# Attention values of one item packed into one PSUM bank, in a two-block decoder on one core

## The reference, cut to what matters

```
scores = einsum('nqhd,nkhd->nhqk', q, k) + bias          # 16 heads of 8 features
attn   = softmax(scores * scale, axis=-1)
out    = einsum('nhqk,nkhd->nqhd', attn, v)               # the part that changes
x      = layernorm(x + out.reshape(n, q, 128) @ Wo.T + bo)
```

## Time and profile before

| What | Value |
|---|---|
| Time, median of 3 runs | 1018.94 us (1016.09, 1018.94, 1019.32) |
| Profiled execution, span | 1016.3 us; the profile gives nothing around it |
| Granted TensorE clock over the span | 0.839 |
| TensorE matmul busy | 787.6 us, 77% of the span |
| VectorE busy | 628.6 us, 62% |
| ScalarE busy | 508.2 us, 50% |
| GpSimd busy | 182.5 us, 18% |
| Context transposes (line 662) | 272, 60.3 us busy |
| Evacuations (line 704) | 144, 51.9 us busy |
| Reciprocals (line 768) | 68, 17.3 us busy |

### The profile page before, as it was taken

The page is one execution under the profiler, slowest core; times in us unless marked ns, Lnnn a source line. Parts: engine busy times, 40 slices in busy tenths (PEclk is TensorE's granted clock), DMA queues, the critical chain, the costliest instruction groups (busy, mean ns, idle before and its releaser), DMA issues.

```text
span 1016.3 us, 20624 instructions
## 1 busy us (share of the span) xinstructions
PE 787.6 (77%) x7086; PEld 426.8 (42%) x7109; DVE 628.6 (62%) x2000; ACT 508.2 (50%) x867; POOL 182.5 (18%) x313
## 2 busy tenths in 40 slices
PE   2787898889996638866659999559999846999960
PEld 1232333444443414443413334313333435999950
DVE  2587987676755814246268994368887345555567
ACT  1157786556564312406417876506566524666630
POOL 2241211011110201001301110121000032602324
PEclk8698998999997765767658999659999957999985
DMA  5466541322120222001522210152110151212212
GB/s 131 114 203 177 155 119 49 115 64 64 51 81 1 63 63 50 2 1 47 140 63 71 73 35 2 37 132 68 51 49 3 57 216 40 90 48 60 75 46 66
DMA packets 76074, 75.57 MB, mean 74 GB/s; under 512 B 21376, under 2 KB 65152, under 8 KB 75216
## 3 DMA queue, kind: packets, MB, share of 16 engines
q1 hardware_dynamic: 73504, 67.18, 23.3%
q0 software_dynamic: 2480, 7.21, 2.1%
HBM read 50.66 MB, written 23.13 MB: 73 GB/s over the span
## 4 chain that ended last, share of the span: by engine, by line
PE 62%; DVE 18%; issue 6%; ACT 4%; POOL 4%; DMA 4%; SPq 2%; POOLq 0%; DVEq 0%; ACTq 0%
PE PS L648 12%; PE PS L582 12%; PE PS L1807 8%; PE PS L599 7%; DVE MS L753 5%; PE PS L662 4%; PE PS L1817 4%; PE PS L589 3%; PE PS L326 2%; POOL experts_x L1718 1%; PE PS L1012 1%; DVE Y L748 1%; DVE CX L770 1%; ACT X L1047 1%; PE PS L173 1%
## 5 line engine op out<-in xcount | busy, mean ns | idle before, releaser
L753 DVE TENSOR_REDUCE MS<-PS 128x2 f32<-128x512 f32 (+2 forms) x448 | 249.2, 591 | 122.1 <-PE PS L599 68.2
L711 ACT ACTIVATE BIG<-PS 128x1024 f32<-128x1024 f32 (+2 forms) x288 | 260.0, 907 | 85.5 <-PE PS L589 45.2
L582 PE MATMUL PS<-BIG 62*128 62x256 bf16 (+1 forms) x1088 | 205.9, 285 | 91.8 <-DVE MS L753 30.4
L589 PE MATMUL PS<-BIG 64*128 64x256 bf16 (+1 forms) x1088 | 187.1, 273 | 1.3 <-DMA BIG<-MT 1.3
L648 PE MATMUL PS<-BIG,VA 128*32 128x256 f32 (+1 forms) x2176 | 170.1, 386 | 1.8 <-ACT OT L704 1.8
L582 PEld LDWEIGHTS PS<-BIG 62*128 62x128 bf16 x1088 | 68.1, 96 | 235.6 <-issue 120.5
L704 ACT COPY OT<-PS 128x256 f32<-128x256 f32 (+1 forms) x144 | 51.9, 360 | 106.1 <-PE PS L648 106.1
L1807 PE MATMUL PS<-OT,VA 128*128 128x128 f32 x736 | 96.3, 278 | 0.4 <-ACT OT L1864 0.4
L1807 PEld LDWEIGHTS PS<-OT,VA 128*128 128x128 f32 x736 | 91.0, 195 | 0.7 <-ACT OT L1864 0.7
L817 POOL CAST MB<-MS 128x16 bf16<-128x16 f32 (+1 forms) x72 | 16.0, 222 | 383.0 <-DVE MS L753 191.8
L648 PEld LDWEIGHTS PS<-BIG,VA 128*32 128x32 f32 x2176 | 43.8, 110 | 73.6 <-issue 63.2
(11 more groups left out here) (223 smaller groups left out, 1091.8 us busy)
## 6 DMA issues: line engine op xcount, KB each, us to landing
rows_q<-parts SPq DMA_DIRECT2D x32, 192.0 KB, 2.1
rows_k<-parts SPq DMA_DIRECT2D x32, 192.0 KB, 2.1
BIG<-rows_q SPq DMA_DIRECT2D x64, 96.0 KB
BIG<-rows_k SPq DMA_DIRECT2D x64, 96.0 KB
BIG<-in_ex_w SPq DMA_DIRECT2D x3, 2048.0 KB, 11.8
BIG<-rows_q SPq DMA_DIRECT2D x64, 64.0 KB
BIG<-rows_k SPq DMA_DIRECT2D x64, 64.0 KB
OT<-experts_x SPq DMA_DIRECT2D x46, 64.0 KB
```

What stands on the lines that cost most here:

```text
L582: return nc.tensor.matmul(bank[:, first:first + kw], g.Q6[b.buf][rows, u, qt * P:(qt + 1) * P], g.K6[b.buf][rows, u, 0:kw], start=start, s ...
L589: return nc.tensor.matmul(g.bank[2 * (v % 2) + a][:, core.offset[kt]:core.offset[kt] + n], g.K6[b.buf][rows, v, kt * P:(kt + 1) * P], g.Q6 ...
L711: nc.scalar.activation(g.PT[v // 2 % 2][:, 2 * (v % 2):2 * (v % 2) + 2, 0:w], g.bank2[v % 2][:, :, 0:w], ACT.Exp, scale=SCALE).then_inc(se ...
L753: nc.vector.tensor_reduce(g.MS[:, 0:n, a, u], self.ring_bank["mx", step, a][:, 0:n * w] .rearrange("p (n k) -> p n k", n=n), axis=AX_X, op ...
```

## The change

`values` now writes group `grp` with `q, o = divmod(grp, 2)`. `o` picks the half of bank 6's columns. `q` picks the half of the 32 partitions: the heads 8 to 15 of `VA` have their 9 filled columns at 16 to 24 of the 32, where heads 0 to 7 have zeros, so groups 2 and 3 are accumulated on the same columns as groups 0 and 1. Only the very first matmul of an item starts the accumulation. One copy evacuates the whole bank per item; only group 0 of the next item waits for it. The transposes are 2 per block of queries, 4 for an item, in steps 0 and 1. The context is one step per item: one reciprocal of 32 (16 in f0), then one multiply per block of queries. The order of heads in V's columns is changed on the host (`VFIRST`) to fit.

```diff
 def contexts(self, no):
-        return self.g.line.cx_done.at(self.items[no].cx + self.nqt)
+        return self.g.line.cx_done.at(self.items[no].k + 1)
 def turns_of(self, items, step):
         k, n = divmod(step - self.LAG - 14, 8)
-        b = self.item(items, k)
-        qt, half = {0: (0, 0), 1: (0, 1), 3: (1, 0), 4: (1, 1)}.get(n, (2, 0))
-        return (b, qt, half) if b and qt < b.core.nqt else (None, 0, 0)
+        return (self.item(items, k), n) if n < 2 else (None, 0)
 # values
-                after(pe, self.ot_done, n)
+                if grp == 0:
+                    after(pe, self.ot_done, b.k)
             lo, w = core.queries[kt]
+            q, o = divmod(grp, 2)
             for hh in range(4):
                 last = nc.tensor.matmul(
-                    g.bank[6][PVW * hh:PVW * hh + PVW, lo:lo + w],
-                    g.VA[b.par][:, kt, 8 * (hh % 2) + 2 * grp + hh // 2, :],
+                    g.bank[6][PVW * hh:PVW * hh + PVW, S * o + lo:S * o + lo + w],
+                    g.VA[b.par][:, kt, 8 * q + 4 * (hh % 2) + 2 * o + hh // 2, :],
                     g.PT[grp % 2][:, hh, core.offset[kt]:core.offset[kt] + w],
-                    start=kt == 0, stop=kt == core.nqt - 1)
+                    start=grp == 0 and kt == 0, stop=grp == 3 and kt == core.nqt - 1, skip_group_check=True)
-        def turn_context(b, qt, half):
-            if half == 0:
-                pe.wait_ge(*self.ot_done.at(4 * b.k + 4))
-                self.bank7(pe, self.cx_done.at(b.cx + qt + 1))
-            for grp in (2 * half, 2 * half + 1):
-                last = nc.tensor.transpose(g.bank[7][:, grp * P:(grp + 1) * P], g.OT[b.par][:, grp, qt * P:(qt + 1) * P],
-                                           g.ident[:, :])
-            if half == 1:
+        def turn_context(b, qt):
+            if qt == 0:
+                pe.wait_ge(*self.ot_done.at(b.k + 1))
+                self.bank7(pe, self.cx_done.at(b.k + 1))
+            if qt >= b.core.nqt:
+                return
+            for o in range(2):
+                last = nc.tensor.transpose(g.bank[7][:, (2 * qt + o) * P:(2 * qt + o + 1) * P],
+                                           g.OT[b.par][:, o, qt * P:(qt + 1) * P], g.ident[:, :])
+            if qt == b.core.nqt - 1:
                 last.then_inc(self.cxt_ready.sem, 1)
-        def evacuate(n):
-            act.wait_ge(*self.pv_done.at(n + 1))
-            if grp == 0 and b.k >= 2:
-                after(act, self.cxt_ready, self.items[b.k - 1].cx)
+        def evacuate(b):
+            act.wait_ge(*self.pv_done.at(4 * b.k + 4))
+            after(act, self.cxt_ready, b.k - 1)
             w = b.core.nqt * P
-            nc.scalar.copy(g.OT[b.par][:, grp, 0:w], g.bank[6][:, 0:w]).then_inc(self.ot_done.sem, 1)
+            nc.scalar.copy(g.OT[b.par][:, 0:2, 0:w], g.bank[6].rearrange("p (o t) -> p o t", o=2)[:, :, 0:w])\
+              .then_inc(self.ot_done.sem, 1)
-            if v % 2 == 0:
-                evacuate(v // 2 - 2)
+            if v % 8 == 2 and self.item(items, v // 8 - 1):
+                evacuate(self.items[v // 8 - 1])
-        def context(b, qt):
+        def context(b):
+            nqt = b.core.nqt
+            dve.wait_ge(*self.cxt_ready.at(b.k + 1))
+            sums = g.bank[7][:, 0:nqt * H * W2].rearrange("p (n w) -> p n w", w=W2)
+            rsum = g.rsum[:, 0:nqt * H]
+            nc.vector.reciprocal(rsum, sums[:, :, DH]).then_inc(self.chain.sem, 1)
+            dve.wait_ge(*self.chain.at(b.k + 1))
+            for qt in range(nqt):
+                heads = slice(qt * H, (qt + 1) * H)
+                last = nc.vector.tensor_tensor(
+                    g.CX[:, b.no * nqt + qt, :].rearrange("p (d s r) -> p r s d", d=DH, r=4),
+                    sums[:, heads, 0:DH].rearrange("p (r s) d -> p r s d", s=4),
+                    rsum[:, heads].rearrange("p (r s) -> p r s", s=4).unsqueeze(3).to_broadcast([P, 4, 4, DH]), ALU.mult)
+            last.then_inc(self.cx_done.sem, 1)
 # value_rows, GpSimd
+            for q in range(2):
+                heads = slice(8 * q, 8 * q + 8)
+                to = g.VA[b.par][:, 0:nqt, heads, W2 * q:W2 * q + DH]
+                if bias is None:
+                    last = nc.gpsimd.tensor_copy(to, v[:, :, heads, :])
+                    continue
+                row = bias.rearrange("p (d h) -> p h d", d=DH)[:, heads, :]
                 for n in range(nqt):
-                    last = nc.gpsimd.tensor_tensor(to[:, n, :, :], v[:, n, :, :], row, ALU.add)
+                    last = nc.gpsimd.tensor_tensor(to[:, n, :, :], v[:, n, heads, :], row, ALU.add)
+            last.then_inc(self.va_ready.sem, 1)
 # start of the program, GpSimd
             for buf in g.VA:
-                last = nc.gpsimd.memset(buf[:, :, :, DH:DH + 1], 1.0)
+                for q in range(2):
+                    last = nc.gpsimd.memset(buf[:, :, 8 * q:8 * q + 8, W2 * q + DH:W2 * q + DH + 1], 1.0)
 # host: the columns of the V weights, of a1's V bias and of ctx
+VFIRST = DFIRST.reshape(DH, 2, 2, 4).transpose(0, 2, 1, 3).reshape(-1)
```

More of the change, by code:

```diff
@@ L48 @@
 PVW = 32
+W2 = PVW // 2
 NPARTS = 4
@@ L510, in __init__ @@
         self.feat_total = [0] * NBUF
-        self.cx_total = self.joins = 0
+        self.joins = 0
         self.bank7_read = None
@@ L538, in add @@
             self.feat_total[b.buf] += 16 * core.loads(no)
-            b.feat, b.cx, b.joins = self.feat_total[b.buf], self.cx_total, self.joins
-            self.cx_total += core.nqt
+            b.feat, b.joins = self.feat_total[b.buf], self.joins
             self.joins += 2 if core.causal else 0
@@ L686, in tensor @@
                 turn_m(b, half)
-            b, qt, half = self.turns_of(items, step)
+            b, qt = self.turns_of(items, step)
             if b:
-                turn_context(b, qt, half)
+                turn_context(b, qt)
             if side:
@@ L778, in vector @@
                     join(bm, step % 8 // 4)
-            b, qt, half = self.turns_of(items, step)
-            if b and half == 1:
-                context(b, qt)
+            b, turn = self.turns_of(items, step)
+            if b and turn == 1:
+                context(b)
             if side:
@@ L796, in value_rows @@
             b.core.values_ready(pool, b.no)
-            to = g.VA[b.par][:, 0:nqt, :, 0:DH]
             v = b.core.values[:, b.no * nqt:(b.no + 1) * nqt, :].rearrange("p t (d h) -> p t h d", d=DH)
-            if bias is None:
-                nc.gpsimd.tensor_copy(to, v).then_inc(self.va_ready.sem, 1)
-            else:
-                row = bias.rearrange("p (d h) -> p h d", d=DH)
+            for q in range(2):
[5 more added lines that the diff above has]
+                row = bias.rearrange("p (d h) -> p h d", d=DH)[:, heads, :]
                 for n in range(nqt):
-                    last = nc.gpsimd.tensor_tensor(to[:, n, :, :], v[:, n, :, :], row, ALU.add)
-                last.then_inc(self.va_ready.sem, 1)
+                    last = nc.gpsimd.tensor_tensor(to[:, n, :, :], v[:, n, heads, :], row, ALU.add)
+            last.then_inc(self.va_ready.sem, 1)
         def parts_of_m(b, half):
@@ L1994, in allocate @@
         self.MT = [sb(f"MT_{i}", [16, S], BF16) for i in range(2)]
-        self.rsum = sb("rsum", [P, H])
+        self.rsum = sb("rsum", [P, 2 * H])
         self.fbuf = [sb(f"fbuf{i}", [P, CH]) for i in range(2)]
@@ L2600, in layout @@
     for n in w:
-        w[n] = w[n][DFIRST] if n in ("a0_qa", "a0_qb", "a0_ka", "a0_kb") else w[n][DFIRST][:, DFIRST]
+        w[n] = w[n][DFIRST] if n in ("a0_qa", "a0_qb", "a0_ka", "a0_kb") else w[n][DFIRST][:, VFIRST if n[3:] == "v" else DFIRST]
     io["weights"] = np.stack([w[n] for n in WEIGHTS], axis=1)
@@ L2606, in layout @@
     rows = {"a1_bv": a["L1_attn_bv"], "a1_bo": a["L1_attn_bo"], "x1_bo": a["L1_xattn_bo"]}
-    io["rowvecs"] = np.repeat(np.stack([rows[n][DFIRST] for n in ROWVECS])[None], P, axis=0)
+    io["rowvecs"] = np.repeat(np.stack([rows[n][VFIRST if n == "a1_bv" else DFIRST] for n in ROWVECS])[None], P, axis=0)
     io["router"] = np.repeat(a["L0_ffn_w_router"][DFIRST][:, None], P, axis=1)
@@ L2624, in layout @@
     io["xt"] = io["x"].T
-    io["ctx"] = a["ctx_1024"].reshape(T, D)[:, DFIRST]
-    io["ctxt"] = io["ctx"].T
+    ctx = a["ctx_1024"].reshape(T, D)
+    io["ctx"], io["ctxt"] = ctx[:, VFIRST], ctx[:, DFIRST].T
     return io
```

3 lines of the change are left out of this document (removed).

## The result

The changed kernel takes 1012.57 us (median of 20 runs, 1007.24 to 1019.92) against 1019.32 (20 runs, 1014.57 to 1029.36) for the kernel before: ratio 0.9935, interval [0.9914, 0.9956]. That is 6.7 us faster where 24 were forecast, outside the range. The profiled execution spans 1008.1 us, the one before 1016.3: two single executions, 8.2 us apart.

A forecast was written before the change was run, and what follows sets the result against it. TensorE was taken to bound the attention stages, sharing a1 with VectorE. Transposes 15.6, context 1.5 and tails 7.8, less 1.0 for the evacuation wait, gave 23.9 us off the 1018.94 median: 995 us, range 985 to 1007.

The forecast's parts named there:

- Transposes: In the attention stages and f0, halving the transposes takes off half of line 662's share of the chain: 15.6 us.
- Context on VectorE: One reciprocal of 32 columns at 0.27 us replaces two of 16; half its chain share in a1 and x1 saves 1.5 us.
- Evacuation wait: In a0 and a1, group 0 waits for a longer copy: 0.06 us charged to each of 16 items, 1.0 us lost.
- Tails: After a stage's last item nothing hides its chain; it gets shorter by 2.4 in a1 and x1, 2.8 in x0: sum 7.8 us.
- What else moves: nothing: GpSimd's value copies, memsets at the start, weight column order and the context's move to step 1 cost nothing.
- A: Transposes are hidden in the streams and only x0 pays in full: 13.7 us off, 1005 us; chance 0.20.
- B: All 25.2 us of transpose pairs pay, with VectorE's savings and tail waits: 33.5 us off, 985 us; chance 0.13.
- C: TensorE's clock falls, some 1.2 us per fallen step; half of a1's 64 steps would give 1033 us; chance 0.04.
- D: The one copy becomes a wait at every item, 0.8 us each, 29 us: 1023 us; chance 0.03.
- Its own signs: Expected in the profile: 136 transposes, 36 copies, reciprocal near 0.27 us, line 662's shares halved, x0's and x1's steps 3 and 4 0.37 shorter.

The follow-up runs named there:

- pairs_back: The changed kernel with its two pairs of transposes done again, unread, at steps 3 and 4 of every item: 1020.9 us, ratio 1.0014 to the kernel before.
- short_values: The changed kernel with value matmuls over half their columns in the eight items of x0 (L0 cross-attention), wrong numbers there: 1009.29 us.
- context_split: The changed kernel with an item's transpose pairs in steps 1 and 4 and a context of 16 sums behind each: 1012.13 us, ratio 0.9911 to the kernel before.
- recip_twice: The changed kernel with the reciprocal of every item's sums taken twice, the first unread: 1014.83 us, ratio 0.9961 to the kernel before.

## Why the prediction was wrong

- *Transposes, 15.6 us: the step that failed.* "Only what is on the chain counts" is true, but a chain share was taken as time that goes when the work goes. pairs_back prices them at 2.6 in x0 (forecast 5.4), 2.9 in a1 (1.8), 3.9 in x1 (3.6), and below nothing in f0 with its approach (1.8). So 12.6 us outside a0 were forecast, and 9.4 less 2.8 is what the two profiles give them. In x0 one of the two pairs of an item that went stood in a step where another loop of 1.67 us, VectorE's maxima and TensorE's answer, is as long (short_values), and the other gave 0.25. The sizes for a1 and x1 had a second fault: the windows of the earlier trace rows are 78 and 100 us long, the streams 100.6 and 119.6. Over the whole streams of the kernel before, line 662 has these shares of the chain in x0, a1 and x1:

```profile
by line: PE PS L599 27.2%; PE PS L648 24.9%; PE PS L582 20.4%; PE PS L662 10.1%; PE PS L589 5.3%; issue 1.5%; PE PS L1061 1.0%; PE PS L1012 0.9%; PE PS L631 0.9%; DVE square L890 0.9%; DVE scale L891 0.9%; DVE square L889 0.9%; DVE MS L753 
by line: PE PS L648 28.7%; PE PS L582 27.2%; DVE MS L753 15.6%; PE PS L589 7.6%; PE PS L662 5.5%; DVE CX L770 3.7%; issue 3.3%; PE PS L1012 3.1%; PE PS L631 2.3%; DVE rsum L768 1.7%; PE PS L993 1.5%; DVEq L744 0.0%
by line: PE PS L648 25.8%; PE PS L599 22.2%; PE PS L582 17.0%; PE PS L662 7.5%; PE PS L589 7.3%; DVE Y L748 4.4%; DVE HN L748 4.4%; issue 3.2%; PE PS L1012 1.7%; DVE CX L770 1.6%; PE PS L631 1.3%; PE PS L993 1.2%; DVE rsum L768 1.1%; ACT BI
```

  Half of that is 5.9, 2.8 and 4.5 us: near what a1 and x1 gave, and over twice what x0 did. a0's 3.0 is unsettled.
- *Context on VectorE, +1.5 us: the sign failed.* The reciprocal of 32 took 0.36 us, not 0.27, so the block is 0.83 and not 0.73, and it stands in one step: between before and pairs_back, alike but for this and the copies, an item is 0.16 longer in x0 and 0.13 in x1, 0.07 shorter in a1, about 1.8 us in all. Splitting the context again (context_split) takes the same 0.16 and 0.13 off. The 0.27 was called nearest to the copies of the earlier trace rows, and was not: a copy grows by 40% from 128 to 256 columns and by 57% from 256 to 512, the reciprocal grew by 45%.
- *Evacuation wait, -1.0 us: right in kind.* In the page of the profile of the changed kernel TensorE's values wait 2.3 us in all for the copy.

```profile
L648 PE MATMUL PS<-BIG,VA 128*32 128x256 f32 (+1 forms) x2176 | 171.2, 390 | 2.6 <-ACT OT L702 2.3
```

- *Tails, 7.8 us: right, a little small.* 3.1, 2.55, 2.9 for x0, a1, x1 (2.8, 2.4, 2.4); f0's 1.0 was 0.2 in the sum.
- *"What else moves: nothing": failed.* a0's order shifted by under half a microsecond, and a conversion fell behind a GpSimd instruction (some 2.2 us). The way to f0 took 2.2 us more, with the half clock longer there. The experts took 128.9, 129.1 and 129.6 us in the three profiles of the old order, and in 13 profiles of changed orders 128.75 to 133.9, median 131.3. TensorE waits there for single blocks of rows:

```profile
846.99 3.15 DMA OT<-experts_x
...
859.86 1.84 DMA OT<-experts_x
```

  The chain of waits holds none, one and two of them in the three profiles of the old order (0, 1.8 and 4.0 us) and four and five in those of the changed kernel (10.4 and 14.0). Why they are rarer in the kernel before stays open; nothing was tried on it, and recip_twice, a changed order, has none (128.75 us).
- *Rivals.* A (hidden in the streams) was nearest in size but kept 13.7 us, and had it the wrong way round: it let x0 pay in full and a1 not, and x0 paid half of its 5.4 and a1 more than its 1.8. B (all of it pays) was wrong: pairs_back prices its 25.2 us at 8 to 9. C named the clock, and rightly said that a1 and x1 hold theirs (0.97 and 1.00); it looked only where nothing happened. D was wrong: 2.3 us of waits for the copy and not 29.
- *Its own signs.* The counts, the halved shares, the wait for the copy and a1's tail (3.7 us) came as said. The reciprocal didn't (0.36), nor did steps 3 and 4, which were to be 0.37 shorter each: 0.25 and nothing in x0, 0.18 and 0.57 in x1. And VectorE's idle time in the 78 us of a1, which was to change, is 7.7 us where it was 8.1.

## What to carry to other kernels

A share of the chain of waits, taken over the whole stage, is about the most that removing that work gives, and can be twice what it gives (5.9 and 2.6 us in x0): take a steady step, find every loop as long as it (here maxima and scores over two banks), and count only what the next longest loop leaves. Work merged into one block lands in one step, so look at what waits behind that step; merge where nothing hides it (split contexts cost a tail 1.0 to 1.15 us here) and spread it where something does (0.16 us an item in x0). When time is taken out of a stream, a pair of instructions on VectorE and GpSimd that just missed each other can be shifted into each other.

## What the runs showed of the hardware

- Value matmuls that fill 32 of 128 output rows run side by side: two of the four heads left out saved next to nothing (0.41 against 0.43 us for 128 queries). The Trainium skill says so of column tiles ("TensorE: Matmul & The Clock Gate", Part 3); the trace agrees.
- A VectorE instruction can wait for GpSimd for a moment that no semaphore of the program asks for: the conversion of 512 columns takes 0.42 us alone, 0.75, 1.17 or 1.37 when it starts 0.69, 0.27 or 0.07 us behind a GpSimd subtraction of 1.16, so that it ends 0.28 us behind it each time.
- One program has two courses in two places. The first exponential came at 56.5 to 59.2 us in seven profiles and at 61.2 to 63.7 in nine, from f0 to a1 it took 96.0 to 98.2 us in four and 101.7 to 102.5 in twelve, with unchanged code; nothing was tried on either. At some 5 us each they could make, by estimate, 10 of the 15 us over which single runs of the kernel before spread; only the profiled runs show their course, so this isn't shown.
